# A graph attention layer on one core: the hand-over from the projections to the attention sums is rearranged

## The reference

```python
h = jnp.maximum(_layernorm(x, axis=-1), 0.0)
# the layer, on h:
h = h @ W.T
src, dst = h @ a1, h @ a2
e = jax.nn.leaky_relu(src[:, None] + dst[None, :], negative_slope=0.2)
e = jnp.where(adj == 0, -9e15, e)
return x + jax.nn.softmax(e, axis=1) @ h
```

## Time and profile before

| | us |
|---|---|
| median of 3 runs (lowest, highest) | 383.94 (383.19, 384.04) |
| profiled execution | 384.0 |
| its span, first to last instruction | 382.4 |
| TensorE busy | 376.6 (98%) |
| VectorE busy | 362.8 (95%) |
| ScalarE busy | 195.7 (51%) |
| GpSimd busy | 43.1 (11%) |
| granted clock of TensorE | 1.00 in every part |

### The profile page before, as it was taken

The page is one execution under the profiler, slowest core; times in us unless marked ns, Lnnn a source line. Parts: engine busy times, 40 slices in busy tenths (PEclk is TensorE's granted clock), DMA queues, the critical chain, the costliest instruction groups (busy, mean ns, idle before and its releaser), DMA issues.

```text
span 382.4 us, 9231 instructions
## 1 busy us (share of the span) xinstructions
PE 376.6 (98%) x3358; PEld 330.5 (86%) x3358; DVE 362.8 (95%) x456; ACT 195.7 (51%) x272; POOL 43.1 (11%) x68
## 2 busy tenths in 40 slices
PE   8999899999999999999999999999999999999996
PEld 6788688888888888888888888888888888888885
DVE  4999999999999999999999999999987999999965
ACT  5999754744443644344445543444446443444430
POOL 3897020000000001110000002100000011100001
PEclk9999999999999999999999999999999999999999
DMA  7931476857676666776666667766665567666503
GB/s 252 374 78 42 136 228 223 278 165 233 221 222 215 210 218 221 235 231 224 220 218 205 216 209 234 239 222 222 216 208 184 169 216 244 232 219 225 171 2 111
DMA packets 27025, 78.23 MB, mean 205 GB/s; under 512 B 3956, under 2 KB 9336, under 8 KB 27000
## 3 DMA queue, kind: packets, MB, share of 16 engines
q1 hardware_dynamic: 25568, 74.59, 60.4%
q0 software_dynamic: 1280, 3.16, 2.2%
q10 hardware_dynamic: 152, 0.13, 0.1%
HBM read 73.66 MB, written 4.21 MB: 204 GB/s over the span
## 4 chain that ended last, share of the span: by engine, by line
PE 96%; ACT 1%; DMA 1%; issue 1%; DVE 0%; ACTq 0%
PE ps L1435 88%; PE ps L1259 2%; PE ps L1274 2%; PE ps L1285 2%; PE ps L1280 2%; DMA a_rows<-a 1%; PE ps L1224 1%; PE ps L1240 1%; ACT c_row L517 0%; ACT h_sb L491 0%; DVE rows_sb L1153 0%; ACT L643 0%; ACT p_hi L527 0%; ACTq L502 0%; PE ps L1234 0%
## 5 line engine op out<-in xcount | busy, mean ns | idle before, releaser
L1435 PE MATMUL ps<-v_sb,p_hi 128*128 (+2 forms) x2048 | 251.9, 273 | 1.0 <-ACT p_hi L527 0.9
L537 ACT ACTIVATE p_hi<-p_sb,gp 128x1024 f16<-128x1024 f32 x126 | 144.4, 1149 | 166.5 <-DVE p_sb L816 140.0
L1435 PEld LDWEIGHTS ps<-v_sb,p_hi 128*128 128x128 f16 x2048 | 199.6, 98 | 26.9 <-issue 1.2
L823 DVE SCALAR_TENSOR_TENSOR p_lo<-p_sb,gp,p_hi 128x1024 f16<-128x1024 f32 x126 | 160.7, 1277 | 7.2 <-ACT p_hi L537 6.7
L816 DVE SCALAR_TENSOR_TENSOR p_sb<-c_row,gp,adj_sb 128x1024 f32<-128x1024 uint32 (+1 forms) x126 | 160.5, 1278 | 0.0
L1435 PE MATMUL ps<-v_sb,p_lo 128*128 (+1 forms) x1024 | 141.6, 273 | 0.0
L1435 PEld LDWEIGHTS ps<-v_sb,p_lo 128*128 128x128 f16 x1024 | 100.0, 98 | 12.8 <-DVE p_lo L823 0.2
L467 POOL DMA_DIRECT2D out<-rows_sb x24 | 13.0, 541 | 263.0 <-DVE rows_sb L1117 262.9
L416 POOL TENSOR_SCALAR hn_sb<-x_sb,moments,rstd 128x256 f32<-128x256 f32 x17 | 21.3, 1260 | 4.1 <-DVE rstd L765 3.2
L775 DVE SCALAR_TENSOR_TENSOR hnt_lo<-ps,hnt_hi 128x256 f16<-128x256 f32 x32 | 12.9, 410 | 0.3 <-ACT hnt_hi L507 0.2
L1274 PE MATMUL ps<-w_hi,hnt_hi 128*128 128x258 f16 x64 | 12.5, 277 | 0.4 <-ACT h_sb L491 0.4
(11 more groups left out here) (87 smaller groups left out, 87.9 us busy)
## 6 DMA issues: line engine op xcount, KB each, us to landing
adj_sb<-adj_t SPq DMA_DIRECT2D x128, 512.0 KB, 4.8
x_sb<-x SPq DMA_DIRECT2D x7, 512.0 KB, 8.5
out<-rows_sb POOLq DMA_DIRECT2D x24, 128.0 KB, 4.6
c_row<-c_flat SPq DMA_DIRECT2D x3, 512.0 KB, 6.7
out<-rows_sb SPq DMA_DIRECT2D x7, 128.0 KB, 1.8
x_sb<-x SPq DMA_DIRECT2D x2, 256.0 KB, 3.5
...
```

Source lines behind the costliest of these rows:

```text
L537: nc.scalar.activation(p_hi[:, u % R, :], p_sb[:, u % R, :], ACT.Copy, scale=p_scale[:, bass.ds(t, 1)])\
L823: nc.vector.scalar_tensor_tensor(out=p_lo[:, u % R, :], in0=p_sb[:, u % R, :], scalar=p_scale[:, bass.ds(t, 1)], in1=p_hi[:, u % R, :], op ...
L1435: return nc.tensor.matmul(ps[:, k, 0:width], part[:, u % R, k * P:(k + 1) * P], v_sb[:, bass.ds(t, 1), v, 0:width], start=start, stop=stop ...
```

## The change: what it does

Seven edits, all within a few microseconds of the hand-over.

1. `table_ready` goes ahead of `keep_h(27)`, straight behind the high part of tile 31.
2. `LATE` is 5: tiles 0 to 26 go into `d_up`, and tiles 27 to 31 are spread in two steps, 27 to 29 into bank 4 (384 columns) and 30, 31 into bank 5 (256 columns). The turned `d_up` lies beside the first in bank 4, so that `d_top` is one reduction of 512 columns and `d_last` one of 256.
3. Tiles 30 and 31 are projected into banks 4 and 5, once both reductions have been made, and no longer wait for tiles 28 and 29 to be kept. The sums' waits follow.
4. `gp_args` is gone. `exp_g` and `exp_p` take the dst column of `h_sb` itself, with a scale and a bias (`p_bias` is one new VectorE instruction on one column; GpSimd makes a fourth scale early on).
5. VectorE keeps tiles 28 and 29.
6. `c_row` of the first group is made by two exponentials of 256 and 768 columns, not four of 256.
7. On VectorE `split_hn_lo(31)` goes behind `p_bias`, `d_most` and `d_up` go ahead of the low parts of tiles 29 and 30, and `value_lo(10)` goes to after the low part of tile 6.

```diff
-    LATE = 4
+    LATE = 5
+    SPREAD = 3
+    EXP_PARTS = ((0, 2), (2, 8))
-    KEPT_BY_VECTOR = []
-    KEPT_BY_SCALAR = list(range(0, T))
+    KEPT_BY_VECTOR = [28, 29]
+    KEPT_BY_SCALAR = list(range(0, 28)) + [30, 31]
+        own_banks = {T - 2: bank_d, T - 1: bank_e}
+        def h_in_psum(t):
+            return ps[:, own_banks.get(t, bank_h + t % 2), 0:FW]
...
-            def exp_gp(tiles, n):
-                act.wait_ge(gp_args_ready, n)
-                nc.scalar.activation(gp[:, :, tiles], gp_args[:, :, tiles], ACT.Exp).then_inc(gp_ready, 1)
+            def exp_g(t0, t1):
+                act.wait_ge(c_bias_ready, 1)
+                act.wait_ge(*kept(t1 - 1))
+                nc.scalar.activation(g_col[:, t0:t1], h_sb[:, t0:t1, F + 1], ACT.Exp,
+                                     bias=exp_bias[:, 0:1], scale=exp_scale[:, 1:2]).then_inc(g_ready, 1)
+
+            def exp_p(t0, t1):
+                act.wait_ge(p_bias_ready, 1)
+                act.wait_ge(*kept(t1 - 1))
+                nc.scalar.activation(p_scale[:, t0:t1], h_sb[:, t0:t1, F + 1], ACT.Exp,
+                                     bias=p_bias[:, 0:1], scale=exp_scale[:, 3:4]).then_inc(p_scale_ready, 1)
...
             split_hn_hi(31)
+            nc.scalar.activation(table_ready[:], eps_sb[:], ACT.Exp)
             keep_h(27)
-            nc.scalar.activation(table_ready[:], eps_sb[:], ACT.Exp)
-            keep_h(28)
+            exp_g(0, R)
             exp_c(0)
-            keep_h(29)
-            exp_gp(slice(0, R), 1)
+            exp_p(0, R)
             exp_c(1)
-            exp_c(2)
             hi_part(0, 0)
-            exp_c(3)
             hi_part(0, 1)
             keep_h(30)
+            keep_h(31)
             hi_part(0, 2)
-            keep_h(31)
...
+            def keep_h(t):
+                dve.wait_ge(h_done, t + 1)
+                nc.vector.tensor_scalar(h_sb[:, t, :], h_in_psum(t), H_DOWN, None, ALU.mult).then_inc(h_kept_vector, 1)
...
             value_lo(8)
-            split_hn_lo(29)
             dve.wait_ge(h_kept, SOON - 1)
             nc.vector.tensor_reduce(d_most[:], h_sb[:, 0:SOON - 1, F + 1], AX.X, ALU.max).then_inc(d_most_ready, 1)
-            split_hn_lo(30)
-            split_hn_lo(31)
+            split_hn_lo(29)
             dve.wait_ge(h_kept, SOON)
...
-            dve.wait_ge(d_all_spread, 1)
-            nc.vector.tensor_reduce(d_top[:], ps[:, bank_d, 0:LATE * P], AX.X, ALU.max).then_inc(d_top_ready, 1)
-            dve.wait_ge(d_turned, 1)
-            nc.vector.tensor_reduce(d_early[:], ps[:, bank_e, 0:P], AX.X, ALU.max).then_inc(d_early_ready, 1)
+            split_hn_lo(30)
+            dve.wait_ge(d_some_spread, 1)
+            dve.wait_ge(d_turned, 1)
+            nc.vector.tensor_reduce(d_top[:], ps[:, bank_d, 0:(SPREAD + 1) * P], AX.X, ALU.max).then_inc(d_top_ready, 1)
+            dve.wait_ge(d_all_spread, 1)
+            nc.vector.tensor_reduce(d_last[:], ps[:, bank_e, 0:(LATE - SPREAD) * P], AX.X, ALU.max).then_inc(d_last_ready, 1)
...
-            nc.vector.tensor_scalar(gp_args[:, 0, 0:R], h_sb[:, 0:R, F + 1], exp_scale[:, 1:2],
-                                    exp_bias[:, 0:1], ALU.mult, ALU.add).then_inc(g_args_ready, 1)
-            dve.wait_ge(g_args_ready, 1)
-            nc.vector.tensor_scalar(gp_args[:, 1, 0:R], gp_args[:, 0, 0:R], 0.25, math.log(P_UP), ALU.mult, ALU.add)\
-                .then_inc(gp_args_ready, 1)
-            value_lo(10)
+            nc.vector.tensor_scalar(p_bias[:], exp_bias[:], 0.25, math.log(P_UP), ALU.mult, ALU.add).then_inc(p_bias_ready, 1)
+            split_hn_lo(31)
+            keep_h(28)
             weights_part(0, 0)
+            keep_h(29)
             weights_part(0, 1)
...
             def project_hi(t):
                 pe.wait_ge(hnt_hi_ready, t + 1)
-                if t >= 2:
+                if t in own_banks:
+                    pe.wait_ge(d_top_ready, 1)
+                    pe.wait_ge(d_last_ready, 1)
+                elif t >= 2:
                     pe.wait_ge(*kept(t - 2))
...
             turn(31)
+            spread_d(ps[:, bank_d, 0:SPREAD * P], SOON, SOON + SPREAD, d_some_spread)
             project_hi(27)
+            turn_d()
+            spread_d(ps[:, bank_e, 0:(LATE - SPREAD) * P], SOON + SPREAD, T, d_all_spread)
             project_w_lo(27)
             project_lo(27)
-            spread_d()
             project_hi(28)
             project_w_lo(28)
-            turn_d()
             project_lo(28)
```

More of the change, by code:

```diff
@@ L142, in gat_layer @@
         d_top = sb("d_top", [P, 1])
-        d_early = sb("d_early", [P, 1])
+        d_last = sb("d_last", [P, 1])
         d_safe = sb("d_safe", [P, 1])
-        gp_args = sb("gp_args", [P, 2, T])
+        p_bias = sb("p_bias", [P, 1])
         gp = sb("gp", [P, 2, T])
@@ L490, in keep_h @@
                 act.wait_ge(h_done, t + 1)
-                nc.scalar.activation(h_sb[:, t, :], ps[:, bank_h + t % 2, 0:FW], ACT.Copy, scale=H_DOWN)\
+                nc.scalar.activation(h_sb[:, t, :], h_in_psum(t), ACT.Copy, scale=H_DOWN)\
                     .then_inc(h_kept, 1)
@@ L663, in _ @@
                 .then_inc(c_col_ready, 1)
-            exp_gp(slice(R, T), 2)
-            act.wait_ge(gp_ready, 2)
+            exp_g(R, T)
+            exp_p(R, T)
+            act.wait_ge(p_scale_ready, 2)
             split_hi(3, 3, 0)
@@ L993, in _ @@
             low_part(1, 0)
-            all_kept(dve)
-            dve.wait_ge(c_bias_ready, 1)
-            nc.vector.tensor_scalar(gp_args[:, 0, R:T], h_sb[:, R:T, F + 1], exp_scale[:, 1:2],
-                                    exp_bias[:, 0:1], ALU.mult, ALU.add).then_inc(g_args_ready, 1)
             edge_weights(2, 2, 16, 0)
@@ L1019, in _ @@
             split_lo(6, 6, 0)
+            value_lo(10)
             dve.wait_ge(p_lo_ready, 5)
@@ L1273, in project_hi @@
                 for c in range(KC):
-                    nc.tensor.matmul(bank_of(t), turned("hi", t)[:, c, :], w_hi[:, c, 0:FW], start=(c == 0), stop=False)
+                    nc.tensor.matmul(h_in_psum(t), turned("hi", t)[:, c, :], w_hi[:, c, 0:FW], start=(c == 0), stop=False)
             def project_w_lo(t):
@@ L1279, in project_w_lo @@
                 for c in range(KC):
-                    nc.tensor.matmul(bank_of(t), turned("hi", t)[:, c, :], w_lo[:, c, 0:FW], start=False, stop=False)
+                    nc.tensor.matmul(h_in_psum(t), turned("hi", t)[:, c, :], w_lo[:, c, 0:FW], start=False, stop=False)
             def project_lo(t):
```

57 lines of the change are left out of this document (27 added, 30 removed).

## The result

The kernel after takes 385.04 us (median of 22 runs, 384.27 to 387.08), the kernel before 384.14 us beside it (22 runs, 383.19 to 385.39). The ratio is 1.002, with an interval from 1.0011 to 1.0029: 0.4 to 1.1 us slower, 0.9 in the middle. The profiled executions span 383.3 and 382.4 us. The forecast was 383.5 and its range ended at 384.4, so the result lies outside.

What follows compares the result with a forecast made beforehand. TensorE's long busy part was a fixed price, and the end followed VectorE's low part of tile 2: 0.11 + 0.29 = 0.40 earlier. 384.0 less 0.40 is 383.6, and 0.06 above the median gives 383.5; range 382.9 to 384.4.

Steps and rivals of the forecast that it cites:

- the one on `value_lo(10)`: VectorE, first group: the row, 0.69 long, moved behind tile 6 costs nothing, as VectorE is 0.9 ahead by then.
- The term that was mis-sized: ScalarE behind the bias: `exp_g` and `exp_p` of four columns, 0.20 each as for `exp_gp`, of which 0.10 shows.
- The 0.11 that I took for `d_most`: VectorE ahead of the bias: `d_most` takes 0.11 from start to start, estimated from `d_up` to `d_top`.
- the 0.37: At the hand-over: `exp_bias` ends at 37.80 instead of 38.17, 0.37 us earlier.
- The second part of the weights: VectorE: starts at 39.59 after waiting for the second exponential, instead of 39.70, so 0.11 earlier.
- The cover of the keeps: VectorE waits 0.24 before the second part of the weights, so each keep may cost 0.12 more at no loss.
- The two late `gp_args`: VectorE behind the second part: two `gp_args` of 28 columns go, 0.21 and 0.08, together 0.29 gained.
- my own signs of being wrong: Bias at 38.1 or later, a keep above 0.5, VectorE idle behind 40 us, or TensorE idle behind 50 us.
- VectorE becomes the wall: Rival, between bias and second part of the weights: dearer keeps or no bias gain give 383.8 to 384.2; chance 0.13.
- The further gain: Rival at the hand-over: bias early and cheaper exponential or reductions gain 0.64, or 0.8 with an earlier turn; chance 0.17.
- The load's drain: Rival on ScalarE: held behind the table load for a second 1.28, 0.56 slower, 384.5; chance 0.03.
- Nothing moves: Rival: the long chain absorbs the change if an unseen TensorE wait behind 50 us sets the end; chance 0.05.

Runs made afterwards that it cites:

- b_extra: Kernel before with one more `value_lo` on VectorE, into a spare buffer, behind the low part of tile 6: 384.54 us, ratio 1.0012 to the kernel before.
- a_args: Kernel after with g and p of the first four source tiles made as before, by two `gp_args` and one exponential: 384.12 us, ratio 1.0006 to the kernel before.
- b_direct: Kernel before with only the late 28 tiles' g and p made directly by exponentials, without their two `gp_args`: 383.82 us, ratio 0.9994.
- a_three: Kernel after with the exponential of 768 columns split into 256 and 512: 384.29 us, ratio 1.0009 to the kernel before.

## Why the prediction was wrong

**The step that failed** is the one on `value_lo(10)`: it "comes back behind tile 6, where its cost is nothing, because VectorE needs some 2.4 us for a source tile (two rows of 1.2) and TensorE 2.64 (24 x 0.11), so that VectorE gains about 0.25 on each tile and is 0.9 ahead by then". The 2.4 and the 2.64 are right, and so is the lead: before, VectorE's low part of tile 6 ended at 58.49 and TensorE's loads of it began at 59.33. A lead at one place is not slack, though, if the row spends it further on. At tile 11 VectorE was 2.05 ahead, at tile 12, behind a `value_lo` and one more row of weights, 0.48, at tile 16 0.24. What I left out is that VectorE's row in the first group has more in it than two rows a tile. The window from 50 us to the end of the group, VectorE's busy time (and number of instructions) before and after:

```profile
50.00:125.30 75.30, 75.28 (x70) 1.00 0.67 221
```
```profile
50.00:125.30 75.30, 75.28 (x71) 1.00 0.69 222
```

It is busy for 75.28 of 75.30 us in both. Before, that is 59 rows of weights and low parts (1.2 each, the first two of group 1 among them), ten `value_lo` (0.60 each) and a transpose. From tile 2 to the low part of tile 16 VectorE wins 14 x 0.24 = 3.4 us on TensorE, and spends 3.1 of them: three `value_lo` (1.8), the transpose (0.1) and one more row of weights that its order puts ahead (1.2). Some 0.3 is left there, and the rows above show 0.24. A fourth `value_lo` does not fit in. By the end of the group the ten have taken 6.0 of the 6.8 us that 28.5 tiles would give, and the first two rows of weights of group 1, 2.4 us, take more than the rest: ScalarE waits 2.55 us for them, and TensorE for ScalarE. `b_extra` shows the price with nothing else changed: 0.62.

With it fell the sentence that the low part of tile 2 "is the last place where TensorE waits for anybody". I had drawn it from the chain, which merged everything behind 42.84 into one piece of TensorE, although I had written that this piece hides small stops. The 0.5 us of waits for `rows_sb` stood in the trace of before. They are not in the list of PE's own waits, which is empty from 50 to 378 us, but in that of its weight loads (PEld).

**The term that was mis-sized** is `exp_g` and `exp_p`, put at "0.20, of which 0.10 shows" each. They show 0.30 and 0.28: 0.38 more in all. I took the price from `exp_gp`, which has no pointer operand, while theirs have two. The Trainium skill (ScalarE: Activation LUTs, What ACT_TABLE_LOAD costs) says in the same section that I weighed for the load that each such operand adds about 93 ns; the rows of after agree, 0.39 against 0.20 for two of them, and I did not use it. `a_args` shows what going back to `exp_gp` and its two `gp_args` is worth to the end, 0.28.

The steps, in order, from the mark:

- The 0.11 that I took for `d_most` is named for `d_up` to `d_top`, which are 0.13 apart; `d_up` came where I had it all the same, 1.04 from the mark (1.05 said). The bias was to end at 3.32 (37.80 - 34.48) and ends at 3.39 (38.11 - 34.72). `d_top` started 0.42 behind the turn's start (36.45 - 36.03) where I had 0.30, and VectorE waited 0.15 for it. Nearly right: 0.30 of the 0.37 were gained.
- `d_last` 0.41, the exponential of 768 columns 1.01 (1.02 said), VectorE's keep 0.42: right, each to 0.01. The table load hidden and without a drain: right, `table_ready` starts 0.02 after the load's end.
- The second part of the weights was to start at 5.11 and started at 5.55. The 0.44 are 0.07 of the bias and 0.38 of `exp_g` and `exp_p`, less 0.01. The cover of the keeps, said to be 0.24, grew to an idle 0.38 for the same reason.
- The two late `gp_args` gave 0.29: right, and `b_direct` shows it alone.
- The low part of tile 2 was to start 0.40 earlier and started 0.03 later (13.11 against 13.08), which is the 0.44 again. TensorE stops in front of the second low part of tile 0, as said, for 0.29 (0.4 said). Tile 29 started at 3.28 (38.00 - 34.72; 3.27 said), and there is no stop of TensorE from there to the end of tile 31, as forecast for the own banks. The first sum came at 6.06 and not at 5.60, because the first high part stands on ScalarE behind the same exponentials.
- Behind that, +0.60 for `value_lo(10)`, forecast at 0. In all 0.44 + 0.60 - 0.40 = 0.64, which is the difference of the ends. Of my own signs of being wrong two came true: VectorE idle behind 40 us (0.38), and a stop of TensorE behind 50 us (0.34).

Had the exponentials cost what I said, the sum would still have been +0.20, as `a_three` shows (+0.21). So the missed price alone gives no change, and the missed lack of slack gives the sign.

**The rivals.** "VectorE becomes the wall" was the right engine. I let it decide only from a second part later than 39.99 and put its place between the bias and that part; it had been the wall all along and up to 125 us, and the price came from another row. From the mark that bound is 5.51, and the second part started at 5.55: the rival's own place explains 0.04 of the loss and no more. The further gain did not occur. The load's drain is not there (`table_ready` at 37.38, the load's end at 37.36). "Nothing moves" had its premise right, an unseen wait of TensorE behind 50 us, and its conclusion wrong: the wait hangs on VectorE, and `b_direct` and `b_extra` move the end by what they change.

**The parts of the change.** Direct g for the late tiles is worth 0.29. The bound's new halves (one tile fewer in `d_up`, two spreads, an earlier turn) bring the bias 0.30 forward: `d_up` waited for the keep of tile 27 before and waits for nothing now. That only pays if VectorE's row gets shorter, and it did not: two keeps of 0.34 each and the wait for `exp_g` and `exp_p` came in for the first `gp_args`. The rows put neither the table load nor the own banks on the way to the bias; they bring tile 29 forward, from 3.94 to 3.28 from the mark, but TensorE then stands idle for 0.64 in front of the first sum, as it did for 0.66 before. No experiment took either apart from the rest, so their single worth is open.
